# Routed experts of a transformer layer: a second row buffer filled by VectorE, registers for the tile table, and last tiles in steps of 64 rows

## The reference

```
probs = softmax(x @ gate_w.T)            # 8 experts, D = 1024
topk_w, topk_i = top_k(probs, 2)         # normalised to sum 1
out  = sum over the 2 chosen experts e of w[e] * ((silu(x @ w_gate[e]) * (x @ w_up[e])) @ w_down[e])
out += sigmoid(x @ sg) * ((silu(x @ sw_gate) * (x @ sw_up)) @ sw_down)     # inner width 1408
```

## Time and profile before

| | us |
|---|---|
| median of 3 runs | 2198.59 (2188.6 to 2212.72) |
| profiled execution, whole | 2196.09 |
| its span, slowest core (7) | 2194.5 |
| spans of cores 0 to 7 | 2175.8, 2192.3, 2156.1, 2181.0, 2141.0, 2149.0, 2170.0, 2194.5 |
| TensorE busy, core 7 | 2028.6 (92%) |
| VectorE, ScalarE, GpSimd busy, core 7 | 787.5, 558.6, 221.0 |

### The profile page before, as it was taken

How to read it: one execution, slowest core, us unless ns; L and a number is a source line. 1 busy time by engine, 2 the same in 40 slices (tenths; PEclk the granted TensorE clock), 3 DMA queues, 4 the chain that set the end, 5 groups by cost and what they waited for, 6 DMA issues and landing times. The chain is left out here.

```text
span 2194.5 us, 37830 instructions; the slowest of 8 cores (2141.0 to 2194.5 us)
## 1 busy us (share of the span) xinstructions
PE 2028.6 (92%) x14222; PEld 1242.7 (57%) x14222; DVE 787.5 (36%) x1942; ACT 558.6 (25%) x964; POOL 221.0 (10%) x194
## 2 busy tenths in 40 slices
PE   4799999984979999999978999999999999999997
PEld 2344444442434444444436767777777777767775
DVE  4367777777425545553511111111111111111111
ACT  1233333321111122112202222322322232222222
POOL 0000000000201110111001111111111111111101
PEclk9899999996989999999998999999999999999999
DMA  9833434436692343224297878778676887878533
GB/s 203 140 97 97 97 97 96 115 62 154 123 207 91 107 155 115 98 98 155 82 194 103 128 115 133 112 128 132 104 131 101 134 134 115 128 120 136 91 55 51
DMA packets 257682, 259.64 MB, mean 118 GB/s; under 512 B 194192, under 2 KB 194448, under 8 KB 255376
## 3 DMA queue, kind: packets, MB, share of 16 engines
q0 software_dynamic: 52320, 140.28, 38.4%
q1 hardware_dynamic: 205232, 117.65, 22.3%
HBM read 220.94 MB, written 83.49 MB: 139 GB/s over the span
## 5 line engine op out<-in xcount | busy, mean ns | idle before, releaser
L1299 PE MATMUL ffn_ps<-r_xT,w 128*128 128x256 bf16 (+1 forms) x6688 | 687.8, 266 | 35.2 <-PEq L1133 35.1
L1299 PEld LDWEIGHTS ffn_ps<-r_xT,w 128*128 128x128 bf16 x6688 | 613.3, 98 | 113.7 <-issue 39.8
L1229 DVE TENSOR_TENSOR r_h<-r_si,ffn_ps 128x256 bf16<-128x256 bf16 (+1 forms) x418 | 165.9, 400 | 879.9 <-DVEq L1133 878.6
L1008 PE MATMUL ffn_ps<-xln2T,w 128*128 128x512 bf16 x1408 | 307.7, 381 | 2.5 <-DVE sh_h L1021 2.5
L1209 ACT ACTIVATE r_si<-ffn_ps 128x256 bf16<-128x256 f32 (+1 forms) x418 | 151.4, 366 | 425.2 <-ACTq L1133 422.2
L334 PE MATMUL att_ps<-xlnT,w 128*128 128x512 bf16 x1024 | 241.5, 386 | 12.1 <-DMA xlnT<-xca 10.5
L1008 PEld LDWEIGHTS ffn_ps<-xln2T,w 128*128 128x128 bf16 x1408 | 137.0, 98 | 166.5 <-issue 5.5
L1257 POOL DMA_INDIRECT out<-r_y,r_meta x70 | 111.0, 1586 | 698.6 <-POOLq L1133 647.7
L334 PEld LDWEIGHTS att_ps<-xlnT,w 128*128 128x128 bf16 x1024 | 96.9, 99 | 129.8 <-issue 20.4
L1309 PE MATMUL ffn_ps<-xca,r_h 128*128 128x512 bf16 x770 | 169.3, 379 | 0.0
L1309 PE MATMUL ffn_ps<-w,r_h 128*128 128x512 bf16 x770 | 169.3, 379 | 0.0
(11 more groups left out here) (144 smaller groups left out, 1111.6 us busy)
## 6 DMA issues: line engine op xcount, KB each, us to landing
xca<-x SPq DMA_DIRECT2D x48, 512.0 KB, 7.4
w<-wu POOLq DMA_DIRECT2D x16, 1408.0 KB, 13.3
w<-wg POOLq DMA_DIRECT2D x8, 2112.0 KB, 15.3
combT_d<-cb SPq DMA_DIRECT2D x8, 1024.0 KB, 5.5
x1b<-x SPq DMA_DIRECT2D x16, 512.0 KB, 7.5
out<-xca SPq DMA_DIRECT2D x16, 512.0 KB, 3.7
out<-x1b SPq DMA_DIRECT2D x16, 512.0 KB, 3.7
xca<-wd POOLq DMA_DIRECT2D x4, 2048.0 KB, 14.9
```

The costliest lines, as they stand in the source:

```text
L1008: i = q.matmul(b_, wslot[w][:, dt * IFF + it * C:dt * IFF + (it + 1) * C], xT2[t % 2][:, dt, :], start=(dt == 0), stop=(dt == 7))
L1229: v.tensor_mul(h[:, it, 0:rt], rsi[:, it % 4, 0:rt], bank(2 + it % 4)[:, RT:RT + rt]).then_inc(r_h, 1)
L1299: i = q.matmul(bank(2 + it % 4)[:, c0:c0 + rt], w_[:, dt * IFF + it * C:dt * IFF + (it + 1) * C], xT[:, dt, 0:rt], start=(dt == 0), stop=( ...
```

## The change

- The transposed rows land in `xTn`. VectorE waits for `r_xfull`, copies all 128 x 2048 elements into `xT`, gives `r_xfree` and then `r_xr`; TensorE waits for `r_xr` in place of `r_xfull` and no longer gives `r_xfree`.
- A spacer `r_skip` moves `ysb` off `x1b`, and ScalarE's wait for `out_stored[1]` goes. VectorE waits for the last scatter, sets `h` to zero and drains before its first tile.
- TensorE, ScalarE and VectorE load the table into 16 registers before the first expert; before, they loaded two registers ahead of each expert.
- The last tile has 64, 128 or 192 rows. Each engine's program has three bodies for it behind the loop, each behind a branch of its own. An expert with up to 192 rows beyond a multiple of 256 gets such a tile. The down matmuls still work on whole groups of 128 rows.
- The table gets a row more, with some 6 more small VectorE operations at the eighth shared tile.

```diff
-    xT = sb2("r_xT", [C, 8, RT], BF16)
+    xTn = sb2("r_xTn", [C, 8, RT], BF16)
     h = sb2("r_h", [C, NIT, RT], BF16)
     rsi = sb2("r_si", [C, 4, RT], BF16)
     meta_f = sb2("r_meta", [C, 2, (ROW - D) // 2], F32)
+    r_skip = sb2("r_skip", [C, 5 * D + 256], F32)
     ysb = sb2("r_y", [C, 2, D], F32)
+    xT = sb2("r_xT", [C, 8, RT], BF16)
...
     def expert_tiles(q):
-        n, full = q.alloc_register("n_tiles"), q.alloc_register("n_full")
+        full = [q.alloc_register("full%d" % e) for e in range(8)]
+        kind = [q.alloc_register("kind%d" % e) for e in range(8)]
         for e in range(8):
-            q.reg_load(n, tbl[0:1, 0, e:e + 1])
-            q.reg_load(full, tbl[0:1, 3, e:e + 1])
-            yield e, n, full
-
-    def tile_loop(q, n, full, tile):
+            q.reg_load(full[e], tbl[0:1, 3, e:e + 1])
+            q.reg_load(kind[e], tbl[0:1, 6, e:e + 1])
+        for e in range(8):
+            yield e, full[e], kind[e]
+
+    def tile_loop(q, full, kind, tile):
         with q.If_ne(full, 0):
             with q.Fori(0, full, 1):
                 tile(RT)
-        with q.If_ne(n, full):
-            tile(RT // 2)
+        for k in range(1, RT // RS):
+            with q.If_eq(kind, k):
+                tile(k * RS)
...
     def act_routed(a):
         wait(a, cnt_tok)
-        wait(a, out_stored[1])
...
     def dve_routed(v):
         wait(v, cnt_tok)
-        for e, n, full in expert_tiles(v):
+        wait(v, sct_tok[NTILE - 1])
+        v.memset(h[:, :, :], 0.0)
+        v.drain()
+        for e, full, kind in expert_tiles(v):
             def tile(rt):
+                take(v, r_xfull, 16)
+                v.tensor_copy(xT[:, :, :], xTn[:, :, :]).then_inc(r_xfree, 1)
+                v.drain().then_inc(r_xr, 1)
                 for it in range(NIT):
...
             def tile(rt):
-                take(q, r_xfull, 16)
+                take(q, r_xr)
...
-                            if hf == 0 and dc == 0 and it == 0:
-                                i.then_inc(r_xfree, 1)
```

More of the change, by code:

```diff
@@ L30 @@
 RT = 256
+RS = 64
 REG = L + RT
@@ L946, in v2 @@
                 if t_cnt is not None:
-                    n, nt, nf, w = (tblf[:, k, :] for k in range(4))
+                    n, nt, nh, w, nf, kd, sm = (tmp[k // 4][:, k % 4, :] for k in range(7))
+                    v.drain()
                     v.tensor_sub(n, base[:, 4, :], ebase)
@@ L966, in v2 @@
                     v.tensor_copy(tbl[:, 1, :], n)
+                    v.tensor_copy(tbl[:, 2, 0:1], sm[:, 0:1])
+                    v.tensor_copy(tbl[:, 6, :], kd)
                     v.drain()
[L968 to L970 removed]
+                    v.tensor_add(w, w, nh)
                     v.drain()
@@ L1123, in emit_ffn @@
     meta_f = sb2("r_meta", [C, 2, (ROW - D) // 2], F32)
+    r_skip = sb2("r_skip", [C, 5 * D + 256], F32)
     ysb = sb2("r_y", [C, 2, D], F32)
+    xT = sb2("r_xT", [C, 8, RT], BF16)
     meta_i = meta_f[:, :, :].bitcast(I32)
-    r_xfull, r_xfree, r_gu, r_si, r_h, r_y, r_yfull, r_yfree, r_mfull, r_mfree, r_expert = (
+    r_xfull, r_xfree, r_xr, r_gu, r_si, r_h, r_y, r_yfull, r_yfree, r_mfull, r_mfree, r_expert = (
         es.enter_context(nc.semaphore("r_" + k)) for k in
-        ("xfull", "xfree", "gu", "si", "h", "y", "yfull", "yfree", "mfull", "mfree", "expert"))
+        ("xfull", "xfree", "xr", "gu", "si", "h", "y", "yfull", "yfree", "mfull", "mfree", "expert"))
     acc = [[sem("r_acc%d_%d" % (hf, e)) for e in range(8)] for hf in range(2)]
@@ L1147, in tile_loop @@
                 tile(RT)
-        with q.If_ne(n, full):
-            tile(RT // 2)
+        for k in range(1, RT // RS):
+            with q.If_eq(kind, k):
+                tile(k * RS)
     def first_rows(s):
-        s.dma_start_transpose(out=xT[:, :, :], in_=dr["xs"].bitcast(BF16)[0:RT, 0:D]
+        s.dma_start_transpose(out=xTn[:, :, :], in_=dr["xs"].bitcast(BF16)[0:RT, 0:D]
                               ).then_inc(r_xfull, 16)
@@ L1192, in sp_routed @@
             take(s, r_xfree)
-            s.dma_start_transpose(out=xT[:, :, :], in_=dr["xs"].bitcast(BF16)[bass.ds(r, RT), 0:D]
+            s.dma_start_transpose(out=xTn[:, :, :], in_=dr["xs"].bitcast(BF16)[bass.ds(r, RT), 0:D]
                                   ).then_inc(r_xfull, 16)
@@ L1202, in act_routed @@
         wait(a, cnt_tok)
-        wait(a, out_stored[1])
         a.sem_inc(r_yfree, 1)
-        for e, n, full in expert_tiles(a):
+        for e, full, kind in expert_tiles(a):
             def tile(rt):
@@ L1212, in tile @@
                 take(a, r_yfree)
-                for hf in range(rt // C):
+                for hf in range((rt + C - 1) // C):
                     for dc in range(2):
@@ L1219, in tile @@
                     a.drain().then_inc(r_yfull, 1)
-            tile_loop(a, n, full, tile)
+            tile_loop(a, full, kind, tile)
     em("scalar", act_routed)
@@ L1230, in tile @@
                                  bank(2 + it % 4)[:, RT:RT + rt]).then_inc(r_h, 1)
-            tile_loop(v, n, full, tile)
+            tile_loop(v, full, kind, tile)
     em("vector", dve_routed)
@@ L1246, in pool_routed @@
         wait(g, out_stored[1])
+        n = g.alloc_register("n_tiles")
         left = g.alloc_register("left")
         half = g.alloc_register("half")
-        for e, n, full in expert_tiles(g):
+        for e in range(8):
+            g.reg_load(n, tbl[0:1, 0, e:e + 1])
             g.reg_load(half, tbl[0:1, 5, e:e + 1])
@@ L1284, in pe_routed @@
         wait(q, v_dn_last)
-        for e, n, full in expert_tiles(q):
+        for e, full, kind in expert_tiles(q):
             sl = 3 * ((e + 1) % 2)
@@ L1312, in tile @@
                                          start=(it == 0), stop=(it == NIT - 1))
-                            if hf == 0 and dc == 0 and it == 0:
-                                i.then_inc(r_xfree, 1)
                         i.then_inc(r_y, 1)
-            tile_loop(q, n, full, tile)
+            tile_loop(q, full, kind, tile)
     em("tensor", pe_routed)
```

25 lines of the change are left out of this document (15 added, 10 removed).

## The result

The changed kernel took 2233.67 us (median of 4 runs, 2222.76 to 2244.96), the kernel before in the same comparison 2194.47 us; the ratio of the paired runs is 1.0177, 95% interval 1.0131 to 1.0222. I had forecast 2215 us and a range of 2186 to 2232. Some executions of every kernel take some per cent longer, with the cores of one die at a lower granted clock; all ratios here leave them out.

A forecast was written before the change was run, and what follows sets the result against it. TensorE was taken to bound the routed stage. On core 1, 2192.3 - 5.8 - 7.0 + 5.6 - 2 + 18.0 + 12.1 = 2213.2; with 1.6 us around the span, 2215 us, range 2186 to 2232.

The forecast's parts named there:

- Three bodies to skip: Behind experts 2, 3 and 6 of core 1, TensorE's skips over unused bodies cost two instruction fetches each time: +18.0 us.
- Behind a last tile: Rows land as late as before, copy and semaphore add 1.4 us, four times on core 1: +5.6 us.
- Between full tiles: Within one expert on core 1, the earlier transposition removes all six TensorE stalls: -7.0 us.
- The first tile: First routed tile, core 1: the wait for the store goes; memset, table loads and copy delay the start: -5.8 us.
- The clock: Gate and up behind seven boundaries of core 1 run slower after idle of 6 us or so: +12.1 us.
- The 192-row tiles: Experts with 129 to 192 rows over save 4.7 us of matmuls, with two skips ahead; core 1 has none.
- The end and the 64-column matmuls: Behind the last expert the shorter tile gains 2 us; 64-column matmuls take 30 ns each.
- three fetches each time: Rival: every skip behind an expert without a last tile fetches instructions, 3 x 3.9 us more, 2227 us; chance 0.28.
- No fetches: Rival: TensorE's skips over unused bodies need no instruction fetch, or the fetches hide; 2190 us; chance 0.17.
- the last tile gains: Rival: rows arrive in time behind last tiles, each boundary 4.6 us shorter; core 1 at about 2182; chance 0.08.

The follow-up runs named there:

- extra_long: The kernel before with one more 128-row last-tile body on every engine, behind a condition that never holds; ratio 1.0096.
- copy: The kernel before with only the second row buffer and VectorE's copy added; ratio 1.0007.
- ahead: The changed kernel with SyncE's loop turned: the next tile's transposition is issued before the wait for GpSimd and the load of row numbers; ratio 1.0170.
- rs128: The changed kernel with last tiles in steps of 128 rows, so one body behind each loop in place of three; ratio 1.0022.
- nested: The changed kernel with one more branch around its three last-tile bodies, so an expert without a last tile makes one jump; ratio 1.0094.
- stage: The kernel before with only the spacer ahead of the buffer of scaled rows and without ScalarE's wait for the last store; ratio 0.9987.
- tail64: The kernel before with its one last-tile body made 64 rows long, no second buffer and no more branches; ratio 1.0029.

## Why the prediction was wrong

**Three bodies to skip: right mechanism, size too small.** This is the step that failed: the term of the jumps, +18.0 us, measured +30.4. I priced m fetches of 3.9 us on 0.7 us of branches, and took m = 2 with 0 and 3 as bounds. Measured at expert 2, three jumps took 4.0, 4.6 and 6.4 us, 15.0 in all, where m = 3 gives 13.8. At expert 3 one of the three took 0.4 us, and there the idle was 8.5 us, where m = 2 gives 6.8. Of the 26 places on the eight cores where an expert has no last tile, 23 have 9.4 to 13.8 us of idle; the other three, expert 3 on cores 1, 2 and 5, have 8.4 to 8.5. In the trace the three jumps hold four packets of instructions at each of experts 2, 3 and 6 of core 1, so even three jumps were not three equal fetches. That a long jump is a fetch, which I had only read out of two rows, is shown now. The branch that I named in the earlier trace rows (L1145) is not the skip, which is L1148's; the price is the same, 4330 against 362 ns. The rows of before did show that a jump is free at three experts of seven; that this would hold for jumps in a row was my guess, and the reason that I gave for rounding up, that nothing can be read ahead within a microsecond, should have led to 3. extra_long shows it: with a second body behind it even the first jump is never free. Why just that jump changes, the runs don't show; the bodies lie elsewhere in the program then. The rule that I cited (Trainium skill, "Runtime: NRT & Kernel Launch", Instruction fetch mechanics: a target outside a window of two pages of 16 KiB is fetched) fits with it, and the packets of 16 KiB inside the long jumps agree; how wide the window is, no run here shows. The 128 KiB that the same section gives TensorE did not keep any three jumps free.

**Behind a last tile: right that nothing is gained, size too small.** I had 1.4 us for copy and semaphore, and the two jumps hidden. Measured: +2.9 per tile. copy has 17.4 us, 1.1 more than before, so the term of the copy was right or a little large. ahead shows the rest: the jumps alone hold TensorE to 17.9. In the changed kernel both end together (copy from 1420.6 to 1421.3, last jump to 1420.8, next branch at 1421.3), and the rows themselves were ready later than before, 7.3 us after their issue against 4.3 (issue in the earlier trace rows, TensorE's start in the earlier trace rows). I worked the jumps out to 9.2 us for two fetches and called them covered; they take 4.2 + 6.3 us at the tile of 1401.94 and start 7.9 us into it. By my own formula two fetches there end 17.7 us into the tile, level with the rows at 17.6, so nothing was in hand.

**Between full tiles: half wrong.** I said that all six stalls go. Four remain on core 1 (0.90, 0.47, 1.88, 0.51). The transposition is issued earlier, as said, but at the moment when GpSimd issues weights, and it is slower there: at 1354.7 its issue takes 11.9 us and the copy can be made at 1372.3, 17.6 us later; before, the one issued at 1378.8 was used at 1389.0. On core 1, 21 of 36 transpositions are now issued within 1.1 us of a weight load, and 19 of these take 9.6 to 12.6 us; before, none was nearer than 7.5 us, and they took 1.4 to 8.0. rs128 and nested have 12 us of such idle. Of the kernels with the second buffer only those with the turned loop have none between full tiles.

**The first tile: right.** First down matmul 33.5 us after the last shared one, before 38.2; the memset took 2.4 us (forecast 2.2), the loads 6.1 (5.5), the copy 0.7 (1.2). For the copy the Trainium skill's 693 ns ("VectorE: DVE Perf Modes") was exact, 693 to 694 ns here, and my nearest row was not near enough. stage adds what I had not seen: with a single buffer the gain was not kept.

**The clock: right.** Seven boundaries, 14.5 us against 15.4.

**The 192-row tiles: not in core 1's sum.** There are three, on cores 0, 3 and 7. From the start of the full tile ahead of it to the next expert it takes 61.9, 56.9 and 62.4 us, where two full tiles took 60.5, 60.2 and 60.5 before: on two of the three the two jumps ahead of the tile cost more than its 64 missing columns save.

**The end and the 64-column matmuls: right.** -2.2 us; 64 matmuls in 2.03 us, about 31 ns each; SiLU holds TensorE for 1.5 us after four blocks.

The rivals: "three fetches each time" had a chance of 0.28 and gave 2227; it is what happened, with the last tiles on top. That the profiled execution took 2227.11 us is luck: core 1's terms came out 10 us dearer than that rival's, its shared stage ended 13.6 us earlier, and another core ended last. "No fetches" and "the last tile gains" are excluded by rows and by extra_long and tail64. My range of 2204 to 2224 for the forecast alone was a little wider than its two bounds give, 2207 to 2223.

## What to carry to other kernels

A branch over a long unused body is work for the engine that it belongs to, and TensorE's bodies are the long ones: count the jumps on the path, nest them behind one condition, and measure one by adding a body that never runs. A shorter tile or a second buffer helps only when the queue that feeds it is free to issue: look for what stands ahead of the next load in its queue (here a wait for another engine, 2.36 us ahead of it every time), and turn the loop. The turned loop was only run together with the second buffer, so what it is worth by itself is open. Parts that are each worth nothing (0.9987, 1.0007, 1.0029) were worth 1.3% together and with the loop turned; by the profiles, each had been waiting for the next.

## What the runs showed of the hardware

- A taken branch of TensorE over 396 or more matmuls and weight loads took 3.0 to 6.4 us when one or two packets of 16 KiB passed on the queue of instructions, and 0.35 to 0.5 us when none did (core 1). Over one instruction it took 0.23 us, and over three bodies at once 3.5 to 4.3 us, no more than over one. The way back to the head of a loop of 440 of them took 0.25 us or less.
- In the kernel before and the changed one, an issue of a 256-row transposition on SyncE's queue of core 1 took 1.4 to 8.0 us when no weight load had been issued in the last 7.5 us, and, with two exceptions, 9.6 to 12.6 us within 1.1 us of one. In stage one took 19.4 us.
- A table load from SBUF into a register takes 0.3 us on TensorE, VectorE and SyncE; 16 in a row took 6.1 us on VectorE.
